# An attention and feed-forward kernel on one core: early loads on one queue, shifts on VectorE, later tiles' terms added down to two slots, new orders

## What is computed

```python
def attention(k, v, q, ssm_kernel, D, head_dim):     # k = v = ctx, q = layernorm(x)
    kv = einsum('bhil,bhjl->bijhl', k, v)
    y = causal convolution of kv with ssm_kernel along l (through FFTs of 2 L), per head h
    out = y + kv * D
    return einsum('bijhl,bhil->bjhl', out, q)
def ffn(x):
    gate, up = silu(x @ Wg.T), x @ Wu.T               # W = (wq - 128) * scale, wq int32
    return (gate * up) @ Wd.T
x = x + attention(ctx, ctx, layernorm(x), ssm_kernel, D, 8)
x = x + ffn(layernorm(x))
```

## Time and profile before

| | us |
|---|---|
| median of 3 runs | 82.05 |
| lowest and highest | 81.99, 83.1 |
| the profiled execution | 81.92 |
| its span | 80.1 |
| TensorE busy in it | 72.2 |
| VectorE busy | 61.1 |
| GpSimd busy | 60.2 |
| ScalarE busy | 46.0 |

### The profile page before, as it was taken

The page is one execution under the profiler, slowest core; times in us unless marked ns, Lnnn a source line. Parts: engine busy times, 40 slices in busy tenths (PEclk is TensorE's granted clock), DMA queues, the critical chain, the costliest instruction groups (busy, mean ns, idle before and its releaser), DMA issues.

```text
span 80.1 us, 1499 instructions
## 1 busy us (share of the span) xinstructions
PE 72.2 (90%) x489; PEld 60.1 (75%) x489; DVE 61.1 (76%) x165; ACT 46.0 (57%) x115; POOL 60.2 (75%) x88
## 2 busy tenths in 40 slices
PE   4955999899999699999999999999999999999620
PEld 3714677488977567979798899887999989889510
DVE  0059459985999989999999987499995784568570
ACT  0410383882394779675699579932755684758400
POOL 4604983999699999999999997999738896064740
PEclk9997589999999999999999999999999999999996
DMA  0699358999999400000000000000400003001013
GB/s 16 134 297 385 114 151 252 384 394 380 248 349 323 152 0 0 0 8 0 0 8 0 0 0 0 0 0 0 135 4 0 0 3 128 8 0 65 0 65 131
DMA packets 7287, 8.28 MB, mean 103 GB/s; under 512 B 976, under 2 KB 6384, under 8 KB 7280
## 3 DMA queue, kind: packets, MB, share of 16 engines
q1 hardware_dynamic: 6368, 7.50, 29.0%
q10 hardware_dynamic: 848, 0.66, 2.9%
q0 software_dynamic: 64, 0.02, 0.1%
HBM read 7.12 MB, written 1.07 MB: 102 GB/s over the span
## 4 chain that ended last, share of the span: by engine, by line
PE 68%; DVE 15%; DMA 6%; POOL 4%; ACT 2%; issue 2%; ACTq 0%; DVEq 0%
PE conv L939 24%; PE down L957 11%; PE turn L890 8%; PE conv L907 7%; PE conv L915 7%; PE conv L917 7%; DMA x_sb<-x 6%; DVE terms L681 3%; PE turn L872 2%; DVE terms L684 2%; PE turn L864 2%; DVE stats_q L636 2%; POOL products L345 2%; DVE terms L260 1%; DVE terms L688 1%
## 5 line engine op out<-in xcount | busy, mean ns | idle before, releaser
L939 PE MATMUL conv<-f_parts,wgu 128*128 128x256 f16 x176 | 23.1, 273 | 0.0
L236 POOL TENSOR_TENSOR h_lo<-hidden,h_hi 128x256 fp32r<-128x256 f32 x18 | 13.5, 753 | 7.6 <-ACT h_hi L484 7.3
L939 PEld LDWEIGHTS conv<-f_parts,wgu 128*128 128x128 f16 x176 | 16.4, 98 | 3.0
L345 POOL TENSOR_TENSOR products<-k_ext 128x512 f32<-128x512 f32 x14 | 17.7, 1278 | 0.8 <-DMA k_ext<-ctx_ext 0.8
L479 ACT ACTIVATE gate_act<-conv,sg_sb 128x256 f32<-128x256 f32 (+1 forms) x24 | 11.3, 471 | 9.9 <-PE conv L939 9.3
L696 DVE SCALAR_TENSOR_TENSOR hidden<-conv,su_sb,gate_act 128x256 f32<-128x256 f32 (+1 forms) x24 | 11.5, 481 | 5.3 <-ACT gate_act L479 5.0
L907 PE MATMUL conv<-products,toeplitz 128*128 128x288 f32 x32 | 11.3, 436 | 0.9 <-DVE products L626 0.8
L915 PE MATMUL conv<-products,toeplitz 128*128 128x288 f32 x32 | 11.1, 429 | 1.0 <-DVE toeplitz L621 1.0
L681 DVE TENSOR_TENSOR terms<-conv,q_ext 128x512 f32<-128x512 f32 x16 | 10.9, 679 | 1.1 <-ACT q_ext L461 1.0
L957 PE MATMUL down<-wd,h_hi 128*128 128x256 f32 x35 | 10.7, 324 | 0.6 <-POOL h_lo L236 0.6
L917 PE MATMUL conv<-products,toeplitz 128*128 128x288 f32 x32 | 10.9, 423 | 0.0
(11 more groups left out here) (61 smaller groups left out, 119.5 us busy)
## 6 DMA issues: line engine op xcount, KB each, us to landing
toeplitz<-taps_pad SPq DMA_DIRECT2D x3, 512.0 KB, 7.9
k_ext<-ctx_ext SPq DMA_DIRECT2D x3, 384.0 KB, 7.2
out<-x_sb SPq DMA_DIRECT2D x8, 128.0 KB, 1.7
wg_int<-wg_t SPq DMA_DIRECT2D x1, 704.0 KB, 6.1
wu_int<-wu_t SPq DMA_DIRECT2D x1, 704.0 KB, 7.4
wd_int<-wd_t SPq DMA_DIRECT2D x1, 640.0 KB, 8.3
x_sb<-x SPq DMA_DIRECT2D x1, 512.0 KB, 8.4
toeplitz<-taps ACTq DMA_DIRECT2D x2, 128.0 KB, 4.4
```

The source lines that it names most:

```text
L236: eng.tensor_tensor(low_of(i, t), hidden[up_lanes(t), i % 2, t, :], high_of(i, t), ALU.subtract).then_inc(done, 1)
L345: nc.gpsimd.tensor_tensor(view(products[:, n:n + 1], GROUP, [[MADE, HALVES], [GROUP, 4], [1, GROUP]]), view(k, 0, [[EXT * B, HALVES], [0, ...
L939: done = nc.tensor.matmul(bank_of(i, t)[:, n, :], wgu[:, c, column:column + P], f_parts[:, i % 2, part, c, :], start=(c == 0 and part == 0 ...
```

## The change

Five things change.

- **Loads.** The taps of heads 0 to 3 are issued by SP, between its own loads, no longer by ScalarE. ScalarE issues skip_all, x of tile 0, and the two small loads that GpSimd issued, then waits for the added taps and stores them. The readback of heads 4..7 is split in two, and the weights' loads go behind k 8..11, x 4..7 and heads 8..11; k 12..15 and heads 12..15 go ahead of the down weights.
- **Taps.** `add_skip_to_taps` moves from VectorE to GpSimd, ahead of `root_q(0)`.
- **Shifts.** The 16 shifts are tensor_scalar instructions of VectorE, as calls of their own (`shift_of_q`, `shift_of_f`), no longer part of GpSimd's roots.
- **Terms.** `TWICE_MERGED` is 3: `merge_last` runs on GpSimd for tiles 3 to 7, and `sum_terms` takes 2 slots there.
- **Orders.** The lists of all engines are ordered anew.

```diff
-TWICE_MERGED = 8
+TWICE_MERGED = 3
...
+    def load_direct(first, last, done):
+        src = bass.AP(taps.tensor, first * (P + L) + 1, [[1, P], [P + L, last - first], [1, L]])
+        sp.dma_start(toeplitz[:, first:last, :], src).then_inc(done, 16)
...
     load_k(0, 1, k_loaded[0])
+    load_direct(0, 1, direct_loaded[0])
     load_k(1, 2, k_loaded[1])
+    load_direct(1, 2, direct_loaded[1])
     load_x(1, 2, x_loaded[1])
     load_k(2, 4, k_loaded[2])
+    load_direct(2, 4, direct_loaded[2])
     load_x(2, 4, x_loaded[2])
     load_k(4, 8, k_loaded[3])
-    sp.wait_ge(taps_ready, 1)
-    sp.dma_start(taps_pad, taps_sb[:, :]).then_inc(taps_stored, 16)
     sp.wait_ge(taps_stored, 16)
-    load_toeplitz(4, 8, toeplitz_loaded[0])
+    load_toeplitz(4, 6, toeplitz_loaded[0])
+    load_toeplitz(6, 8, toeplitz_loaded[1])
+    load_k(8, 12, k_loaded[4])
+    load_x(4, TILES, x_loaded[3])
+    load_toeplitz(8, 12, toeplitz_loaded[2])
     sp.dma_start(wg_int[:, :, :], wg_t.rearrange("(c p) n -> p c n", p=P)).then_inc(wg_loaded, 16)
     sp.dma_start(wu_int[:, :, :], wu_t.rearrange("(c p) n -> p c n", p=P)).then_inc(wu_loaded, 16)
-    load_x(4, TILES, x_loaded[3])
-    load_k(8, 12, k_loaded[4])
-    load_toeplitz(8, 12, toeplitz_loaded[1])
     sp.dma_start(sg_sb[:, :], s_gate).then_inc(scales_loaded, 16)
     sp.dma_start(su_sb[:, :], s_up).then_inc(scales_loaded, 16)
     sp.dma_start(sd_sb[:, :], s_down.partition_broadcast(P)).then_inc(scales_loaded, 16)
+    load_k(12, H, k_loaded[5])
+    load_toeplitz(12, H, toeplitz_loaded[3])
     full = FULL * P
     sp.dma_start(wd_int[:, 0:FULL, :],
                  wd_t[0:full, :].rearrange("(t p) n -> p t n", p=P)).then_inc(wd_loaded, 16)
     for lanes in (gate_lanes(FULL), up_lanes(FULL)):
         sp.dma_start(wd_int[lanes, FULL, :], wd_t[full:HID, :]).then_inc(wd_loaded, 16)
-    load_k(12, H, k_loaded[5])
-    load_toeplitz(12, H, toeplitz_loaded[2])
...
-        wait(pool, q_rstd, t + 1)
-        nc.gpsimd.tensor_scalar(shift_q[:, t:t + 1], moments_q[:, t, 0:1], rstd_q[:, t:t + 1], -1.0,
-                                ALU.mult, ALU.mult).then_inc(q_shift, 1)
     def root_f(t):
         wait(pool, f_variance, t + 1)
         nc.gpsimd.tensor_tensor(rstd_f[:, t:t + 1], variance_f[:, t:t + 1], minus_half[:, :],
                                 ALU.pow).then_inc(f_rstd, 1)
-        wait(pool, f_rstd, t + 1)
-        nc.gpsimd.tensor_scalar(shift_f[:, t:t + 1], moments_f[:, t, 0:1], rstd_f[:, t:t + 1], -1.0,
-                                ALU.mult, ALU.mult).then_inc(f_shift, 1)
+    def add_skip_to_taps():
+        nc.gpsimd.tensor_tensor(taps_sb[:, P:P + 1], taps_sb[:, P:P + 1], skip_sb[:, :],
+                                ALU.add).then_inc(taps_ready, 1)
...
-    nc.gpsimd.dma_start(taps_sb[:, :], taps).then_inc(taps_loaded, 16)
-    nc.gpsimd.dma_start(skip_sb[:, :], skip).then_inc(taps_loaded, 16)
     nc.gpsimd.memset(anti[:, :], 0.0).then_inc(ident_zeroed, 1)
     nc.gpsimd.memset(ident[:, :], 0.0).then_inc(ident_zeroed, 1)
     nc.gpsimd.memset(minus_half[:, :], -0.5).then_inc(half_ready, 1)
...
                             base=1 - P, pattern=[[1, P]], channel_multiplier=1).then_inc(anti_ready, 1)
     nc.gpsimd.affine_select(out=ident[:, :], in_=ident[:, :], compare_op=ALU.not_equal, fill=1.0,
                             base=0, pattern=[[-1, P]], channel_multiplier=1).then_inc(ident_ready, 1)
+    pool.wait_ge(taps_loaded, 32)
+    add_skip_to_taps()
     pool.wait_ge(half_ready, 1)
     root_q(0)
     pool.wait_ge(k_loaded[2], 16)
...
     pool.wait_ge(k_loaded[3], 16)
     pairs(4)
     pairs(5)
+    pairs(6)
     root_q(3)
-    pairs(6)
     pairs(7)
     pool.wait_ge(k_loaded[4], 16)
     pairs(8)
+    root_q(4)
     pairs(9)
     merge_front(nc.gpsimd, 2)
-    root_q(4)
     root_f(0)
+    root_q(5)
     pairs(10)
     root_f(1)
-    root_q(5)
     pairs(11)
+    root_q(6)
     merge_front(nc.gpsimd, 3)
-    root_q(6)
-    root_f(2)
-    merge_front(nc.gpsimd, 4)
-    root_f(3)
     pool.wait_ge(k_loaded[5], 16)
     pairs(12)
+    root_q(7)
+    merge_last(nc.gpsimd, 3)
+    merge_front(nc.gpsimd, 4)
+    root_f(2)
+    merge_last(nc.gpsimd, 4)
+    low(0, 0)
     pairs(13)
-    low(0, 0)
+    root_f(3)
+    merge_front(nc.gpsimd, 5)
+    pairs(14)
+    low(0, 1)
+    merge_last(nc.gpsimd, 5)
     root_f(4)
-    low(0, 1)
-    root_q(7)
     low(0, 2)
-    merge_front(nc.gpsimd, 5)
+    pairs(15)
     low(0, 3)
-    pairs(14)
-    pairs(15)
     low(0, 4)
+    merge_front(nc.gpsimd, 6)
+    root_f(5)
+    merge_last(nc.gpsimd, 6)
     low(1, 0)
-    root_f(5)
+    merge_front(nc.gpsimd, 7)
     low(1, 1)
     low(1, 2)
+    merge_last(nc.gpsimd, 7)
+    root_f(6)
     low(1, 3)
-    merge_front(nc.gpsimd, 6)
+    low(1, 4)
+    root_f(7)
     add(0, 0)
+    low(2, 0)
     add(0, 1)
-    low(1, 4)
-    merge_front(nc.gpsimd, 7)
-    low(2, 0)
-    root_f(6)
     low(2, 1)
     low(2, 2)
-    root_f(7)
     add(1, 0)
-    add(1, 1)
     low(2, 3)
     low(2, 4)
+    add(1, 1)
     low(3, 0)
+    low(3, 2)
     add(2, 0)
-    low(3, 2)
+    add(2, 1)
     low(3, 4)
-    add(2, 1)
     add(3, 0)
...
-    load_direct(0, 1, direct_loaded[0])
+    act.dma_start(skip_all[:, :], skip.rearrange("h a -> (h a)").partition_broadcast(P)).then_inc(skip_loaded, 16)
     act.dma_start(x_sb[:, 0, :], x[0:P, :]).then_inc(x_loaded[0], 16)
-    act.dma_start(skip_all[:, :], skip.rearrange("h a -> (h a)").partition_broadcast(P)).then_inc(skip_loaded, 16)
-    load_direct(1, 2, direct_loaded[1])
-    load_direct(2, 4, direct_loaded[2])
+    act.dma_start(taps_sb[:, :], taps).then_inc(taps_loaded, 16)
+    act.dma_start(skip_sb[:, :], skip).then_inc(taps_loaded, 16)
     nc.scalar.preload_act_table(ACT.Silu)
-    norm_q(0)
+    act.wait_ge(taps_ready, 1)
+    act.dma_start(taps_pad, taps_sb[:, :]).then_inc(taps_stored, 16)
     act.wait_ge(k_loaded[2], 16)
     squares(2)
+    norm_q(0)
+    squares(3)
     evict_q(0)
     norm_q(1)
-    squares(3)
     act.wait_ge(k_loaded[3], 16)
     squares(4)
     squares(5)
...
     wrap(0)
     squares(7)
     evict_q(2)
-    convert_gate()
-    norm_q(3)
     wrap(1)
     act.wait_ge(k_loaded[4], 16)
     squares(8)
     squares(9)
+    norm_q(3)
     squares(10)
+    squares(11)
+    convert_gate()
     wrap(2)
+    norm_q(4)
+    evict_q(3)
     convert_up()
-    evict_q(3)
-    squares(11)
-    norm_q(4)
     act.wait_ge(k_loaded[5], 16)
     squares(12)
+    evict_q(4)
     norm_f(0)
     squares(13)
-    evict_q(4)
-    high_f(0)
     squares(14)
     norm_f(1)
+    high_f(0)
     wrap(3)
+    norm_q(5)
     squares(15)
     high_f(1)
     convert_down()
+    norm_q(6)
+    wrap(4)
+    evict_q(5)
     act.wait_ge(scales_loaded, 3 * 16)
     gate(0, 0)
...
+    def shift_of_q(t):
+        wait(dve, q_rstd, t + 1)
+        dve.tensor_scalar(shift_q[:, t:t + 1], moments_q[:, t, 0:1], rstd_q[:, t:t + 1], -1.0,
+                          ALU.mult, ALU.mult).then_inc(q_shift, 1)
...
-    dve.wait_ge(x_loaded[0], 16)
-    stats_of_q(0)
-    moments_of_q(0)
     dve.wait_ge(anti_ready, 1)
     dve.wait_ge(skip_loaded, 16)
     dve.wait_ge(direct_loaded[0], 16)
     direct(0)
-    variance_of_q(0)
+    dve.wait_ge(x_loaded[0], 16)
+    stats_of_q(0)
     dve.wait_ge(k_loaded[1], 16)
     all_products(1)
-    dve.wait_ge(taps_loaded, 32)
-    add_skip_to_taps()
+    moments_of_q(0)
     dve.wait_ge(direct_loaded[1], 16)
     direct(1)
+    variance_of_q(0)
     dve.wait_ge(x_loaded[1], 16)
     stats_of_q(1)
     moments_of_q(1)
-    variance_of_q(1)
+    shift_of_q(0)
     dve.wait_ge(direct_loaded[2], 16)
     direct(2)
-    multiply_terms(0)
+    variance_of_q(1)
+    direct(3)
     dve.wait_ge(x_loaded[2], 16)
     stats_of_q(2)
     moments_of_q(2)
+    shift_of_q(1)
     variance_of_q(2)
-    direct(3)
+    multiply_terms(0)
+    stats_of_q(3)
+    shift_of_q(2)
     multiply_terms(1)
-    stats_of_q(3)
     moments_of_q(3)
     multiply_terms(2)
     variance_of_q(3)
     multiply_terms(3)
+    dve.wait_ge(x_loaded[3], 16)
+    stats_of_q(4)
+    shift_of_q(3)
+    moments_of_q(4)
+    stats_of_q(5)
+    variance_of_q(4)
     add_sum(0)
+    moments_of_q(5)
     multiply_terms(4)
     stats_of_f(0)
     multiply_terms(5)
+    stats_of_q(6)
     moments_of_f(0)
-    dve.wait_ge(x_loaded[3], 16)
-    stats_of_q(4)
+    variance_of_q(5)
     add_sum(1)
+    shift_of_q(4)
+    moments_of_q(6)
+    stats_of_f(1)
+    variance_of_f(0)
     merge_back(dve, 2)
-    stats_of_f(1)
     moments_of_f(1)
-    moments_of_q(4)
-    variance_of_f(0)
-    variance_of_q(4)
+    variance_of_q(6)
+    multiply_terms(6)
     variance_of_f(1)
-    stats_of_q(5)
-    multiply_terms(6)
     add_sum(2)
-    stats_of_q(6)
-    moments_of_q(5)
-    stats_of_f(2)
     stats_of_q(7)
-    variance_of_q(5)
-    moments_of_q(6)
-    moments_of_f(2)
+    shift_of_f(0)
+    moments_of_q(7)
     multiply_terms(7)
-    variance_of_q(6)
+    shift_of_q(5)
```

(101 more changed lines are left out.)

114 lines of the change are left out of this document (53 added, 61 removed).

## The result

The changed kernel takes 81.81 us (median of 20 runs, 81.38 to 82.26), the kernel before 82.15 us (20 runs, 81.94 to 83.15): a ratio of 0.9947 [0.9922, 0.9971]. The gain is some 0.4 us (0.34 by the medians), where 2.2 were forecast; the time lies outside the range given.

What follows compares the result with a forecast made beforehand. TensorE was taken to bound the kernel from 26.68 us on, after a stage where three engines hand over work. Span 80.1 - 1.2 (front) - 2.18 (matmuls) + 1.2 (new waits) = 77.9 us; median 79.8 us, range 78.4 to 81.6.

Steps and rivals of the forecast that it cites:

- The front: Before TensorE's full stretch: the stretch starts 1.2 us sooner, at about 25.5 us; bounds 0 and 2.3 us.
- the one on SP's early loads: Loads in the front: nine issues before SP's first wait, not six; readback half a us sooner, later weights at no cost.
- The matmuls: Sums of tiles 3 to 7 in the full stretch: four matmuls less per tile, 2.18 us off TensorE.
- New waits: Full stretch, 26.7 to 45 us: VectorE's 18.2 us against TensorE's 17.0, so TensorE waits 1.2 us; bounds 0 and 2.5.
- rival 3: 26.7 to 45 us: VectorE becomes the bound through ten shifts and merges stretched by merge_last; 83.8 us; chance 11%.
- The shifts: 16 shifts on VectorE at 0.147 us each, 2.4 us, no wait; at most 0.25 us each, 4 us.
- GpSimd: Five merge_last at 1.28 us, 6.4 us, against 16 shifts given up, 5.1 us; hidden behind the new order, no cost.
- The room of 0.7 us: Tile 3's sum: merge_last(3) ends at about 33.9 us, TensorE asks at 34.6 us; more room with a lead.
- rival 2: Front: half clock covers convolutions 2 and 3 and takes the front's gain; 81.0 us; chance 9%.
- rivals 1: To 45 us: VectorE sets the pace, the merged terms save nothing there, the front gives half; 80.7 us; chance 16%.

Runs made afterwards that it cites:

- no_readback: `x_next` with the Toeplitz of heads 4 to 15 read from the input, the store's wait behind all SP loads, skip weight of those heads left out; ratio 0.9782.
- once: Changed kernel without the second merge: TWICE_MERGED 8 again, the five merge_last calls gone; ratio to the kernel before 1.0081.
- shifts_pool: Changed kernel with the 16 shifts back in GpSimd's roots; ratio to the kernel before 1.0178.
- before_warm: Kernel before with more filling multiplies, 22 for 17 ahead of convolution 0 and 8 between its parts; ratio 1.003.
- x_next: Changed kernel with the load of x of tiles 4 to 7 right behind the readback of heads 4 and 5; ratio to the kernel before 0.9935.
- k_split: Changed kernel with k of heads 6, 7, then x 4..7 behind the readback of heads 4, 5, and merge_back(6) behind hidden_units(1, 0) and variance_of_f(5); ratio 0.9899.
- x_early: Changed kernel with x of tiles 4 to 7 issued ahead of SP's wait for the taps' store; ratio to the kernel before 1.0037.
- act_back6: Changed kernel with early loads issued by ScalarE and GpSimd as before, and merge_back(6) behind hidden_units(1, 0) and variance_of_f(5); ratio 0.9813, median 80.81 us.
- before_twice: Kernel before with the second merge alone: TWICE_MERGED 3, each merge_last right behind its merge_front on GpSimd; ratio 1.0615, 87.4 us.
- act_next_back6: `act_back6` with x of tiles 4 to 7 also loaded behind the readback of heads 4 and 5; ratio 0.9792, median 80.53 us.

## Why the prediction was wrong

**The front, forecast -1.2 us, measured -0.27 (and +0.5 in the repeated trace, -0.1 by the medians).** The step that failed is the one on SP's early loads: "The readback should start some half a us sooner", and the order of loads at "no cost". It asked for the deadlines of k 4..7 and of the weights, and took the store's landing to follow its issue. The store landed when the loads ahead of it had, and with nine loads on one queue these end later (DMA idle from 9.50 to 10.50 us, before from 9.00): with these loads the readback came 0.4 to 1.2 us later, not half a us sooner. Everything behind the wait for the store slips with it, x of tiles 4 to 7 above all, whose reader the new order had moved ahead; VectorE stood 1.94 us for it. That reader's deadline wasn't looked at.

The work that VectorE has in the front was summed well enough: with the wait for the store out of the way (`no_readback`), the full stretch starts at 25.50 us, the 25.5 us of the forecast. The exact match is luck. There the loads run without a gap, which the forecast did not have, and from 11 to 25.5 us GpSimd is as full as VectorE (14.20 and 14.11 of 14.50 us), which the sum left out.

The rule stood in the Trainium skill: "DMA: Bandwidth & Descriptors", section "Queues, rings and completion order", says that a transfer's semaphore lands only after every earlier write of that DMA engine, on whatever queue. The traces agree as far as they go: they show the release following the idle DMA engines (table above), not the single writes.

**The matmuls, forecast -2.18 us.** Right in count (60) and place. But the second merge is worth 1.1 us net (`once`), since half of it is lost again in the stretch.

**New waits, forecast +1.2 us, measured +1.95.** Within the bounds of 0 and 2.5, but mis-sized, and worked out for the wrong stage. The 1.2 us were VectorE's load from 26.7 to 45 us (18.2 us) less TensorE's 17.0. There VectorE was busy 17.29 us, not 18.2, and TensorE idled 0.19 us. The hole is in the next stage: 0.83 us is one event, merge_back(6) at 1.79 us ahead of hidden_units(1, 0) in VectorE's list. That VectorE would be late was right; that a stretched merge can do it stood under rival 3. Of the 1.95 us, 0.8 come with the new order and 1.1 with the second merge (`once`), and moving that one call gives back 0.5. TensorE's windows show 0.19 + 0.92 = 1.11 us idle; the other 0.84 us lies within rows of matmuls that are longer in the chain than others like them (1.05 us against 0.87 for eight, 0.64 against 0.48 for two), and it was not settled what those are.

**The shifts.** 0.203 us each, not 0.147: 3.3 us for sixteen, inside the bound of 4. What queues behind them waited 0.2 us, as said. Moving them is worth 1.9 us in the new order, more than the sum gave them credit for: it saw the cost on VectorE and the room on GpSimd, but didn't price the two waits that come without that room.

**GpSimd.** Right: 1.28 us each, no wait of TensorE for it, merge_last(3) done at 33.75 us (33.9 forecast) and asked for at 34.61 (34.6); waits for variance_q fell from 4.8 to 1.3 us, and there is none for k_ext after 12 us. The room of 0.7 us was real but thin, as `shifts_pool` shows by a wait of 0.7 us.

**The rivals.** None came about at its price. The clock, rival 2, stayed at 1.00, and `before_warm` shows no gain from holding it up. VectorE did not become the bound of the stage to 45 us (rivals 1 and 3): it was busy 17.29 of 18.30 us, and TensorE idled 0.19 us there. But rival 3's mechanism is in the trace: two merges of VectorE were stretched, to 1.12 and 1.79 us (it reckoned with 1.22), and the second held up TensorE.

**The rest.** Tail -0.11, around the span 1.88 us and not 1.82, and a median 0.43 us above the profiled execution, not 0.13. Together 0.93 + 0.75 - 0.11 + 0.06 + 0.30 = 1.9 of the 2.0 us between forecast and median (79.8 and 81.81 us). The 0.30 us of the median is the front again: this trace's was early.

## What to carry to other kernels

A wait in the queue that issues the loads is a deadline for everything behind it. Look at the DMA share around such a wait: here two empty microseconds ahead of a long full stretch were lost for each later load, and a small store issued sooner didn't shorten them; what helped was issuing the loads ahead of it sooner (0.6 us) or taking the wait out (1.3 us, `x_next` to `no_readback`). When an order on one engine moves a reader forward, check its transfer too, and an early first result is no gain by itself.

## What the runs showed of the hardware that was not expected

- The same small store (24 KB) released its waiter 2.1 to 2.2 us (the three kernels with the front of before, and `k_split`), 3.0 to 3.1 us (ScalarE issuing the taps' loads, new order), 3.4 to 4.5 us (SP issuing all) and 5.0 us (512 KB more ahead, `x_early`) after its issue. Counted from the DMA engines' going idle it was 0.4 to 0.8 us in 16 of 18 traces.
- The same program lands its early loads differently from one execution to the next: the readback of the changed kernel went out at 10.15 and at 10.95 us, from stores issued 0.03 us apart.
- A 128x512 merge on VectorE that starts just behind one on GpSimd took 1.79 to 1.82 us in four traces, against 0.68 us alone.
- The fall of the clock to half in the front (a mean of 0.54 from 7 to 9 us and 0.61 from 9 to 11 us in the kernel before) is in one trace of the others alone, `act_back6` (0.68 and 0.50); `before_twice`, whose front is that of the kernel before, had 1.00. In `act_back6` turn_q(4) came at 26.79 us, against 26.16 in `act_next_back6` with nearly the same readback, so there the clock may have cost something; that stays open.
